# Token stage of an attention and ternary feed-forward layer: QKV units set among the up units, the next tile's norm and transposes set into the down projection

## The reference

```python
xn = _layernorm(x)                                       # (8, 1024, 512), eps 1e-5
qkv = einsum('bld,ed->ble', xn, W_qkv)                   # W_qkv (1536, 512), 16 heads of 32
attn = softmax(Q K^T * 32**-0.5); out = attn V; out @ W_o^T
...
def bitlinear(x, w):                                     # forward value
    return layer_norm(x, eps=1e-6) @ ternarize_weights(w)^T
h = gelu(bitlinear(xn, w_fc))                            # w_fc (2048, 512), exact gelu
ffn = bitlinear(h, w_proj)                               # w_proj (512, 2048)
result = x + attention(xn) + ffn
```

## Time and profile before

| what | us |
|---|---|
| median of 3 runs | 3723.32 |
| lowest and highest | 3719.41, 3723.57 |
| the profiled execution | 3720.91 |
| its span, first to last instruction | 3719.1 |
| token stage in it, TensorE's first up matmul to the end of its last down matmul | 1504.19 |

### The profile page before, as it was taken

The page is one execution under the profiler, slowest core; times in us unless marked ns, Lnnn a source line. Parts: engine busy times, 40 slices in busy tenths (PEclk is TensorE's granted clock), DMA queues, the critical chain, the costliest instruction groups (busy, mean ns, idle before and its releaser), DMA issues. The chain is left out here.

```text
span 3719.1 us, 54043 instructions
## 1 busy us (share of the span) xinstructions
PE 3449.2 (93%) x17648; PEld 1429.0 (38%) x17648; DVE 2407.9 (65%) x3431; ACT 1838.2 (49%) x1922; POOL 2062.9 (55%) x705
## 2 busy tenths in 40 slices
PE   3999999999999999979999999999999999999587
PEld 2444444444444444423333333333333333332366
DVE  6666666666666666667777777777777777774111
ACT  3444444444444444306666666666666666667211
POOL 0322223333332232208888888888888888889422
PEclk7999999999999999969999999999999999999799
DMA  4122222222222222232223223223223323220365
GB/s 158 69 74 91 74 91 74 91 74 91 70 91 71 86 73 87 68 80 61 68 64 74 68 62 77 67 60 79 65 62 79 65 62 71 68 66 28 128 228 201
DMA packets 376012, 308.26 MB, mean 83 GB/s; under 512 B 300672, under 2 KB 317056, under 8 KB 365440
## 3 DMA queue, kind: packets, MB, share of 16 engines
q1 hardware_dynamic: 375744, 304.69, 29.1%
HBM read 96.99 MB, written 139.46 MB: 64 GB/s over the span
## 5 line engine op out<-in xcount | busy, mean ns | idle before, releaser
L908 DVE TENSOR_REDUCE half_maxima<-scores_for_maxima 128x1 f32<-128x512 f32 x2048 | 1347.0, 687 | 417.9 <-PE scores_for_maxima L977 412.5
L871 ACT ACTIVATE probs<-scores,scalars 128x1024 f32<-128x1024 f32 x1024 | 1092.2, 1112 | 666.3 <-PE scores L955 665.6
L839 POOL TENSOR_TENSOR probs_sum<-probs_sum,probs 128x2048 f32<-128x2048 f32 x256 | 1162.3, 4540 | 16.9
L977 PE MATMUL scores_for_maxima<-k_stackT,q_stackT 96*128 96x512 f16 x2048 | 808.3, 395 | 57.9 <-DMA q_stackT<-stack_scratch 11.2
L955 PE MATMUL scores<-q_stackT,k_stackT 98*128 98x512 f16 x2048 | 615.8, 383 | 21.5 <-issue 17.5
L968 PE MATMUL outputs<-probs,v_rows 128*32 128x512 f32 x4096 | 551.4, 611 | 0.8 <-ACT probs L871 0.8
L977 PEld LDWEIGHTS scores_for_maxima<-k_stackT,q_stackT 96*128 96x128 f16 x2048 | 197.2, 96 | 907.5 <-DVE half_maxima L908 777.1
L839 POOL TENSOR_TENSOR probs_sum<-probs 128x2048 f32<-128x2048 f32 x64 | 290.9, 4545 | 336.5 <-ACT probs L871 336.5
L558 ACT ACTIVATE gelu_out<-psA,scalars 128x1024 f32<-128x1024 f32 x128 | 142.5, 1113 | 668.2 <-PE psA L607 668.2
L607 PE MATMUL psA<-x_hi,ternary_fcT 128*128 128x512 f16 x1024 | 389.4, 380 | 1.4 <-DVE x_lo L431 1.4
L607 PE MATMUL psA<-x_lo,ternary_fcT 128*128 128x512 f16 x1024 | 389.3, 380 | 0.0
(11 more groups left out here) (123 smaller groups left out, 3281.4 us busy)
## 6 DMA issues: line engine op xcount, KB each, us to landing
stack_scratch<-hi_hi_lo_hi_rows SPq DMA_DIRECT2D x32, 1536.0 KB, 5.1
stack_scratch<-hi_hi_lo_hi_rows SPq DMA_DIRECT2D x32, 576.0 KB, 5.9
v_scratch<-v_rows_out SPq DMA_DIRECT2D x32, 576.0 KB, 6.9
x_rows<-in_L_attn_x SPq DMA_DIRECT2D x16, 1024.0 KB, 4.8
x_plus_ffn_scratch<-x_rows SPq DMA_DIRECT2D x16, 1024.0 KB, 3.9
v_rows<-v_scratch SPq DMA_DIRECT2D x32, 512.0 KB, 4.0
inverse_denominators<-denominators_scratch SPq DMA_DIRECT2D x256, 64.0 KB, 2.1
attention_scratch<-out_normed SPq DMA_DIRECT2D x64, 256.0 KB, 2.1
```

The source lines that it names most:

```text
L839: nc.gpsimd.tensor_tensor(acc[:, hf], pr[:, 0] if j == 1 else acc[:, hf], pr[:, j], ALU.add).then_inc(added, 1)
L871: nc.scalar.activation(pr[:, w % 8, 2 * hp:2 * hp + 2, :], psS[:, hp], ACT.Exp, scale=keep["scal"]["escale"]).then_inc(exp_done, 1)
L908: nc.vector.tensor_reduce(mx[:, slot(n, 2), h, t, kh:kh + 1], psX[:, r % 2, :], axis=AX.X, op=ALU.max).then_inc(max_done, 1)
L977: nc.tensor.matmul(psX[:, r % 2, :], qT[0:STACK, slot(n, 4), h, t * P:(t + 1) * P], kT[0:STACK, slot(n, 4), h, kh * BANK:(kh + 1) * BANK], ...
```

## The change

The twelve QKV units are dealt to the eight up units by a table: one behind each even j, two behind each odd one. There is no tail any more. The down projection follows the last QKV unit. Behind its first row block stand the hidden sums, behind the second and the third the transposes of the next tile. Hidden sums and transposes now use the banks of psB, the down projection alternates over psC. The first row block waits for h_lo pair by pair (eight waits) in place of one wait ahead of it. VectorE makes the next tile's statistics between the two QKV units of j = 5 and its normed rows behind the two writes of row block 0; GpSimd makes its nine steps behind the fold.

```diff
         VS = 6
+        qkv_of = [(0,), (1, 2), (3,), (4, 5), (6,), (7, 8), (9,), (10, 11)]
...
                                             ALU.add).then_inc(g_added, 1)
-                    if j == 3 and has_next:
-                        norm(shift(t, 1), 1 - s)
                 pool.wait_ge(g_added, lin(t, last_adds, last_adds))
                 nc.gpsimd.tensor_tensor(gacc[:, 0:BANK], gacc[:, 0:BANK], gacc[:, BANK:2 * BANK], ALU.add).then_inc(g_folded, 1)
+                if has_next:
+                    norm(shift(t, 1), 1 - s)
                 pool.wait_ge(var_ready, lin(t, 1, 1))
...
                     dve.wait_ge(xh_ready, lin(t, 4, c + 1))
-                    nc.vector.tensor_tensor(xl[:, s, c, :], psC[:, (1 - s + c) % 2, :], xh[:, s, c, :],
+                    nc.vector.tensor_tensor(xl[:, s, c, :], psB[:, c % 2, :], xh[:, s, c, :],
                                             ALU.subtract).then_inc(xl_ready, 1)
...
                                                    ALU.mult, ALU.subtract).then_inc(hl_ready, 1)
-                    low_qkv(t, s, j)
-                    if j == 2 and has_next:
+                    for u in qkv_of[j][:1]:
+                        low_qkv(t, s, u)
+                    if j == 5 and has_next:
                         stats(shift(t, 1), 1 - s)
-                    if j == 5 and has_next:
-                        normed(shift(t, 1), 1 - s)
-                add_square(t, UNITS1 - 1)
-                fold_squares(t)
-                for u in range(UNITS1, 12):
-                    if u in (8, 10) and has_next:
-                        low(shift(t, 1), 1 - s, (u - 8, u - 7))
-                    low_qkv(t, s, u)
+                    if j == UNITS1 - 1:
+                        add_square(t, j)
+                        fold_squares(t)
+                    for u in qkv_of[j][1:]:
+                        low_qkv(t, s, u)
...
                 dve.wait_ge(st_full, lin(t, 1, 1))
-                nc.vector.tensor_scalar(st[:, 0:2, :], psC[:, (s + 4) % 2, 0:8].rearrange("p (a b) -> p a b", a=2),
+                nc.vector.tensor_scalar(st[:, 0:2, :], psB[:, 0, 0:8].rearrange("p (a b) -> p a b", a=2),
                                         1.0 / F, None, ALU.mult).then_inc(st_out, 1)
...
                     nc.vector.scalar_tensor_tensor(cen, keep["colsum"][:], st[:, 0, i:i + 1],
-                                                   psC[:, (s + 5 + i) % 2, :], ALU.mult, ALU.add).then_inc(cen_ready, 1)
+                                                   psC[:, i % 2, :], ALU.mult, ALU.add).then_inc(cen_ready, 1)
                     dve.wait_ge(cen_ready, lin(t, 4, i + 1))
...
                                                    ALU.mult, ALU.add).then_inc(y_ready, 1)
+                    if i == 0 and has_next:
+                        normed(shift(t, 1), 1 - s)
+                    if i in (1, 2) and has_next:
+                        low(shift(t, 1), 1 - s, (2 * i - 2, 2 * i - 1))
...
                     act.wait_ge(t_full, lin(t, 4, c + 1))
-                    nc.scalar.copy(xh[:, s, c, :], psC[:, (1 - s + c) % 2, :]).then_inc(xh_ready, 1)
+                    nc.scalar.copy(xh[:, s, c, :], psB[:, c % 2, :]).then_inc(xh_ready, 1)
...
                         square(t, j - 1)
-                    evacuate(t, s, j)
-                square(t, UNITS1 - 1)
-                for u in range(UNITS1, 12):
-                    if u in (8, 10) and has_next:
-                        high(shift(t, 1), 1 - s, (u - 8, u - 7))
-                    evacuate(t, s, u)
+                    for u in qkv_of[j][:1]:
+                        evacuate(t, s, u)
+                    if j == UNITS1 - 1:
+                        square(t, j)
+                    for u in qkv_of[j][1:]:
+                        evacuate(t, s, u)
+                if has_next:
+                    high(shift(t, 1), 1 - s, range(CD))
...
                         pe.wait_ge(xl_ready, lin(t, 4, c - 1))
-                    elif not first:
-                        wait(pe, cen_ready, lin(t, 4, c - 5))
+                    elif c == 0 and not first:
+                        pe.wait_ge(st_out, lin(t, 1))
+                    elif c == 1 and not first:
+                        pe.wait_ge(b_out, lin(t, 12))
                     for i in range(4):
-                        last = nc.tensor.transpose(psC[:, (1 - s + c) % 2, i * P:(i + 1) * P],
+                        last = nc.tensor.transpose(psB[:, c % 2, i * P:(i + 1) * P],
                                                    x2[:, i, c * P:(c + 1) * P], keep["id32"][:])
...
                 last.then_inc(b_full, 1)
+
+            def hidden_sums(t):
+                pe.wait_ge(g_folded, lin(t, 1, 1))
+                pe.wait_ge(sq_folded, lin(t, 1, 1))
+                pe.wait_ge(b_out, lin(t, 12, 11))
+                for q, acc in enumerate((gacc, sqacc)):
+                    for i in range(4):
+                        last = nc.tensor.matmul(psB[:, 0, 4 * q + i:4 * q + i + 1],
+                                                acc[:, i * P:(i + 1) * P], keep["ones32"][:, 0:1], start=True, stop=True)
+                last.then_inc(st_full, 1)
...
                     last.then_inc(a_full, 1)
-                    project_qkv(t, s, j)
-
-                for u in range(UNITS1, 12):
-                    if u in (8, 10) and has_next:
-                        transposes(shift(t, 1), 1 - s, (u - 8, u - 7))
-                    project_qkv(t, s, u)
-
-                pe.wait_ge(g_folded, lin(t, 1, 1))
-                pe.wait_ge(sq_folded, lin(t, 1, 1))
-                if has_next:
-                    pe.wait_ge(xl_ready, lin(t, 4, 8))
-                else:
-                    pe.wait_ge(cen_ready, lin(t, 4))
-                for q, acc in enumerate((gacc, sqacc)):
-                    for i in range(4):
-                        last = nc.tensor.matmul(psC[:, (s + 4) % 2, 4 * q + i:4 * q + i + 1],
-                                                acc[:, i * P:(i + 1) * P], keep["ones32"][:, 0:1], start=True, stop=True)
-                last.then_inc(st_full, 1)
-
-                pe.wait_ge(hl_ready, lin(t, UNITS1, UNITS1))
+                    for u in qkv_of[j]:
+                        project_qkv(t, s, u)
+
                 for i in range(4):
-                    if i == 1:
-                        pe.wait_ge(st_out, lin(t, 1, 1))
-                    elif i >= 2:
-                        pe.wait_ge(cen_ready, lin(t, 4, i - 1))
+                    wait(pe, cen_ready, lin(t, 4, i - 1))
                     for f in range(CF):
+                        if i == 0 and f % 2 == 0:
+                            pe.wait_ge(hl_ready, lin(t, UNITS1, f // 2 + 1))
                         for k, h in enumerate((hh, hl)):
-                            last = nc.tensor.matmul(psC[:, (s + 5 + i) % 2, :], h[:, f, i * P:(i + 1) * P],
+                            last = nc.tensor.matmul(psC[:, i % 2, :], h[:, f, i * P:(i + 1) * P],
                                                     keep["t2T"][:, f, :], start=(f == 0 and k == 0),
...
                     last.then_inc(y_full, 1)
+                    if i == 0:
+                        hidden_sums(t)
+                    elif i < 3 and has_next:
+                        transposes(shift(t, 1), 1 - s, (2 * i - 2, 2 * i - 1))
...
```

## The result

The changed kernel takes 3655.17 us (median of 4 runs, 3654.41 to 3655.70) against 3723.16 (median of 4, 3719.41 to 3723.57): a ratio of 0.9819, 95% interval 0.9802 to 0.9836. The forecast was 3654.5. The span of the profiled execution is 3653.9 us against 3719.1, 65.2 less.

What follows compares the result with a forecast made beforehand. TensorE bounds the kernel, busy 1457.3 of 1504.2 us, losing time in the tail. A stage of 1436.8 gains 67.4 on 3720.91: 3653.5, or 3655.9 with the median's 2.4; forecast 3654.5, range 3647 to 3675.

Steps and rivals of the forecast that it cites:

- the loss stands in the tail: Old tile, between up phase and down projection: 18.48 us, of which 4.66 are lost; TensorE is busy throughout elsewhere.
- the sum: Token stage 1436.8 us instead of 1504.2; gain 67.4: waits 46.8, restarts 3.2, clock falls 15.2, small delays 2.2.
- No wait at the QKV units: Up phase: a unit's bank is taken again 6.04 us after its end, 2.59 in the old tail; no wait.
- the step on VectorE's load: Up phase with the spread QKV units: VectorE has at most 42 us of work in 58.7.
- Rival C: VectorE late at unit 11 in the up phase: 0.2 to 1.0 us a tile, 3658 to 3671; chance 0.12.
- the worst case: Unit 9's bank freed 17.45 us after up unit 5 if both VectorE chains collide with GpSimd, 0.2 too late.
- Rival B: Behind the hidden sums, norm at 3.93 instead of 1.91 or GpSimd's steps late: 3673 or 3686; chance 0.10.
- Which unit waits: Old tail: TensorE waits 2.81 us for unit 9's first matmul, until VectorE empties unit 7's bank.
- Clock: Old stage: 9 of 16 tiles have a lower clock behind waits of 2.6 to 2.8 us; none expected after.
- rival D: Pauses inside the down projection throw the clock: 1.69 us each fall, all 46 would make 3732; chance 0.03.
- the move of sums and transposes: Into the down projection: same 1.70 us for sums and 2 x 0.88 for transposes on TensorE, no wait.
- waits already met: The eight waits for h_lo inside row block 0, 0.86 us apart, were taken to cost nothing.

Runs made afterwards that it cites:

- the first two experiments: Changed kernel with QKV units dealt as before: 3727.30 us; changed kernel with next tile's norm and statistics back in the up phase, units spread: 3654.56 us.

## Why the prediction was right, point by point

- **TensorE is the bound and the loss stands in the tail.** Shown: the tile is 89.79 us, the sum said 86.32 + 1.70 + 1.76 = 89.78.
- **The sum.** New stage 1436.8 forecast, 1436.95 measured; gain 67.4 forecast, 67.2 in the stage. The span fell by 65.2 and the median by 68.0: the stages behind it and the runs vary by more than the error of the sum. That the total came within 0.7 us (3654.5 and 3655.17) is partly luck: 3654.5 was chosen between 3653.5 and 3655.9.
- **No wait at the QKV units.** Shown; and that it takes the spreading, and not the move of the norm, by the first two experiments.
- **But the step on VectorE's load was wrong.** The prediction had at most 42 us of work in 58.7; it is 44.89. The same instructions take VectorE 974.3 us in the stage, 926.5 before, 47.8 more. Two groups after, and the second as it was in the stage before (what, count, busy us, mean ns, idle before):

```profile
L455 DVE TENSOR_SCALAR h_hi<-gelu_out,scalars 128x1024 f16<-128x1024 f32 x128 | 186.8, 1460 | 160.2 <-ACT gelu_out L561 156.6
...
L441 DVE TENSOR_TENSOR square_sum<-square_sum,gelu_squared 128x1024 f32<-128x1024 f32 x96 | 206.9, 2155 | 13.4 <-ACT gelu_squared L528 13.4
```

```profile
L440 DVE TENSOR_TENSOR square_sum<-square_sum,gelu_squared 128x1024 f32<-128x1024 f32 x96 | 155.8, 1623 | 1.5 <-ACT gelu_squared L525 1.0
```

The squares' sum takes 2155 ns instead of 1623 and h_hi 1460 instead of 1285. Both meet GpSimd. A squares' sum that overlaps no large GpSimd instruction takes 1.21 us in either kernel; 79 of all 112 overlap one now, at 2.64 on the mean, and 73 did before, at 2.06. The cause read from the trace: VectorE is hardly late any more. In the median tile it takes up a gelu output 0.03 us after it is made, for seven of the eight up units, and GpSimd starts its addition 0.1 later; before, it came 2.7, 4.3 and 3.0 us late at units 3, 6 and 7. The spreading and the move of the norm each bring a part: VectorE is busy for 951.3 us of the stage with the norm back in the up phase, and for 954.9 with the spreading undone. I had taken the work as fixed and only removed and added instructions. It cost nothing since 13.8 us of 58.7 were still left.
- **Rival C, unit 11.** VectorE's statistics, and the instruction that frees unit 9's bank (it ends at 518.54):

```profile
509.72 2.46 DVE L403 BATCH_NORM_STATS2 bn<-x_rows 128x6 f32<-128x512 f32 x4
...
517.80 0.74 DVE L425 SCALAR_TENSOR_TENSOR hi_hi_lo_hi_rows<-psB,qkv_scale,hi_hi_lo_hi_rows 128x512 f16<-128x512 f32 x1
```

Counted back from 522.40 with 3.45 and 2.59 a unit, unit 11 starts at 519.81 and up unit 5 ended at 502.55. The bank is free 15.99 us after that, where 17.45 was the worst case and 17.26 the deadline: 1.27 early. The worst case had both chains at 6.25; the one behind the statistics (513.14 to 518.54) takes 5.40, because VectorE comes late to it and only h_hi meets GpSimd's addition (2.41, the squares' sum behind it 1.21).
- **Rival B, 0.8 us to spare at the transposes.** Right to a tenth: 7.81 against 8.61 in the trace, and 0.74 to 0.84 hidden with three instructions more. The terms given for the start of the norm add up to T + 5.8 where 5.85 was written and 5.90 measured.
- **Which unit waits.** The prediction told the tail by one tile, where it is unit 9. In eight of the sixteen tiles of the kernel before most of the wait stands at unit 8, behind the first transposes, for unit 6's bank:

```profile
621.34 1.04 PE L583 MATMUL psC<-id,x_normed 128*128 128x128 f32 x8
624.97 0.44 PE L593 MATMUL psB<-wqkvT_hi,x_hi 128*128 128x512 f16 x1 [2.60 <-DVE hi_hi_lo_hi_rows L424]
```

The sum went by the total of the waits and did not notice; the account of the cause was that of some of the tiles.
- **Clock.** Right that the falls go with the waits, and that pauses of the size of the sums and transposes make none: rival D had 46 such pauses a run, and the clock of the stage is 1.00. By the Trainium skill's "TensorE: Matmul & The Clock Gate", section "A second HAM failure mode: psum-queue depth-cycling", small pauses between groups of matmuls can make the clock go to and fro. That has no case here: small groups between dense ones had no lower clock where no wait stood beside them (46 a run) or one of 0.8 us (15).
- **The rest of the moves.** I had costed the move of sums and transposes at nothing and did not say what they would cost if left: 145 and 128 us against the changed kernel. Nor did I see that the waits for h_lo one by one are needed: I called them waits already met, and they are, but the one wait that they replace would not have been.

## What to carry to other kernels

Where an engine waits for a bank, compare the time between a bank's filling and its next use with the time that the emptying chain takes at that point, lateness included; here, dealing work of two kinds evenly bought that distance at no cost to TensorE. When such a spreading takes away work that covered a wait, look at what then stands next in the engine's order: here it had to depend only on what was done several us before. A step that is moved for the sake of a loaded engine may be worth nothing, which one run with it alone put back tells.

## What was not expected of the hardware

The same VectorE instructions took 974.3 us in the stage instead of 926.5, as more of them ran beside GpSimd's additions: the squares' sum 2155 ns on the mean instead of 1623, and the norm 1.91 us for its four instructions away from GpSimd, 3.93 beside it. In this kernel the engine that is on time is busier than the one that was late. And a fall of the clock cost more the longer the wait: about 1.7 us behind waits of 2.6 to 2.8 us, where full matmuls follow, some 4 us where the wait was 5.0 us and the eight small sums followed it. There the clock stayed low for 8 us after the wait. Which of the two, the wait or the sums, makes the difference, no run tells.
